# Wavelet mix on one Trainium2 core: the early unit's second products and edges run on one row half of the array beside projections on the other

## What is computed

```python
x: (8, 512, 207, 64)                      # batch, time, node, channel
a = x.transpose(0, 2, 3, 1).reshape(-1, 512)
for _ in range(3):                        # 8-tap filters, stride 2
    a, d = _dwt(a); details.append(d)
coeffs = [a] + details[::-1]
enh = [c * w[i] per channel for i, c in enumerate(coeffs)]
rec = enh[0]
for d in enh[1:]:
    rec = _idwt(rec[:, :d.shape[-1]], d)  # back to 512 samples
return x + rec(as b, t, n, c) @ proj_w.T + proj_b
```

## Time and profile before

| | |
|---|---|
| median of three runs | 2358.09 us |
| the profiled execution | 2359.12 us, its span 2357.3 us |
| PE busy | 2342.1 us (99% of the span) |
| PE weight loads busy | 2189.6 us (93%) |
| DVE busy | 1750.1 us (74%) |
| ACT busy | 1830.6 us (78%) |
| POOL busy | 284.2 us (12%) |
| a group in the middle of the run | 11.18 us |

### The profile page before, as it was taken

One profiled execution on the slowest core, in us unless ns is written; L12 is line 12 of the kernel. 1 busy time (PEld: TensorE's weight loads), 2 busy tenths in 40 slices (PEclk: granted clock), 3 DMA queues, 4 the chain that ended last, 5 costly groups with the idle time before them and its releaser, 6 DMA issues.

```text
span 2357.3 us, 85222 instructions
## 1 busy us (share of the span) xinstructions
PE 2342.1 (99%) x33980; PEld 2189.6 (93%) x33980; DVE 1750.1 (74%) x2920; ACT 1830.6 (78%) x3938; POOL 284.2 (12%) x1051
## 2 busy tenths in 40 slices
PE   9999999999999999999999999999999999999998
PEld 8999999999999999999999999999999999999987
DVE  5777777777777777777777777777777777777766
ACT  5777777777777777777777777777777777777776
POOL 1111111111111111111111111111111111111110
PEclk9999999999999999999999999999999999999998
DMA  3545454454644645444454644645445454544643
GB/s 127 219 184 191 178 201 173 182 212 162 242 162 162 233 172 199 180 188 186 178 203 170 235 162 162 241 163 210 183 174 198 178 192 182 222 162 167 237 162 122
DMA packets 107209, 439.42 MB, mean 186 GB/s; under 512 B 6801, under 2 KB 8081, under 8 KB 106898
## 3 DMA queue, kind: packets, MB, share of 16 engines
q1 hardware_dynamic: 106144, 434.16, 48.9%
q10 hardware_dynamic: 754, 0.28, 0.0%
HBM read 217.33 MB, written 217.06 MB: 184 GB/s over the span
## 4 chain that ended last, share of the span: by engine, by line
PE 98%; DVE 0%; issue 0%; DMA 0%; ACT 0%; ACTq 0%; DVEq 0%
PE proj_ps L436 31%; PE coefs_ps L382 31%; PE synth_ps L465 12%; PE synth_ps L477 11%; PE synth_ps L488 6%; PE proj_ps L446 2%; PE synth_ps L479 2%; PE synth_ps L467 2%; PE synth_ps L490 2%; DMA edge_sb<-edge_m 0%; DVE x_sb L676 0%; DVE proj_lo L656 0%; DVE coefs_sb L650 0%; ACT stack_sb L602 0%; ACTq L552 0%
## 5 line engine op out<-in xcount | busy, mean ns | idle before, releaser
L382 PEld LDWEIGHTS coefs_ps<-analysis_sb,x_sb 64*128 64x128 f32 x13200 | 945.5, 188 | 102.2 <-DVE coefs_sb L650 53.4
L382 PE MATMUL coefs_ps<-analysis_sb,x_sb 64*128 64x84 f32 x13200 | 1009.9, 270 | 2.7 <-DVE coefs_sb L645 1.5
L436 PE MATMUL proj_ps<-w_sb,coefs_sb 64*128 64x64 f32 x13248 | 871.3, 271 | 1.2 <-issue 1.2
L656 DVE TENSOR_TENSOR proj_lo<-proj_ps,proj_hi 128x512 fp32r<-128x512 f32 x828 | 568.1, 686 | 370.0 <-ACT proj_hi L571 370.0
L436 PEld LDWEIGHTS proj_ps<-w_sb,coefs_sb 64*128 64x128 f32 x13248 | 815.9, 189 | 1.4 <-issue 1.3
L650 DVE TENSOR_TENSOR coefs_sb<-coefs_ps,scale_sb 128x552 f32<-128x552 f32 x825 | 602.4, 730 | 207.6 <-PE coefs_ps L382 206.7
L571 ACT ACTIVATE proj_hi<-proj_ps 128x512 fp32r<-128x512 f32 x828 | 472.1, 596 | 174.6 <-PE proj_ps L446 157.4
L589 ACT ACTIVATE stack_sb<-proj_hi 20x512 fp32r<-20x512 f32 x621 | 390.9, 629 | 209.1 <-DVE proj_lo L656 204.1
L676 DVE TENSOR_TENSOR x_sb<-synth_ps,x_sb 128x512 f32<-128x512 f32 x828 | 531.7, 684 | 16.7 <-PE synth_ps L490 6.9
L341 POOL TENSOR_TENSOR coefs_sb<-coefs_sb 128x20 f32<-128x20 f32 x828 | 187.8, 227 | 1893.4 <-DVE coefs_sb L650 1892.7
L589 ACT ACTIVATE stack_sb<-proj_lo 20x512 fp32r<-20x512 f32 x621 | 390.4, 629 | 15.0
(11 more groups left out here) (58 smaller groups left out, 2849.1 us busy)
## 6 DMA issues: line engine op xcount, KB each, us to landing
x_sb<-x SPq DMA_DIRECT2D x182, 1152.0 KB, 11.7
out<-x_sb SPq DMA_DIRECT2D x182, 1152.0 KB, 6.3
out<-x_sb SPq DMA_DIRECT2D x1, 1280.0 KB, 4.7
x_sb<-x SPq DMA_DIRECT2D x1, 1024.0 KB, 8.5
out<-x_sb SPq DMA_DIRECT2D x2, 512.0 KB, 2.9
x_sb<-x SPq DMA_DIRECT2D x1, 768.0 KB, 5.7
x_sb<-x SPq DMA_DIRECT2D x1, 512.0 KB, 4.0
stack_sb<-bias_parts SPq DMA_DIRECT2D x12, 2.0 KB, 2.7
```

The lines of the kernel that those rows point to most:

```text
L382: return lambda cols: nc.tensor.matmul(out[:, at:at + HALF_COLS], x_sb[half_rows[side], w, cols], analysis_sb[half_rows[side], :], start=s ...
L436: mm = nc.tensor.matmul(out_cols[:, :, p, :], coefs_of(g, p)[rows, own_cols(w)], w_sb[rows, rows].rearrange("k (h c) -> k h c", h=2), star ...
L656: nc.vector.tensor_tensor(proj_lo[w][:, :].rearrange(by_node, n=2), proj_of(w)[:, :, 0:NODE_COLS], proj_hi[w][:, :].bitcast(fp32).rearrang ...
```

## The change

A new function, `synthesise_across(turn, g, half, behind)`, is called twice in a group, where `synthesise_second` of the early unit and the projections of windows 0 and 1 stood. A call makes the early unit's three second products and two edge products on row half `half`, and between them all eight matmuls that project windows 0 and 1 for node `1 - half`, which lie on the other half's rows. The second call does the same with the roles exchanged. `analyse_first` of pair 2 stands between the calls, `analyse_second` of pair 2 behind the second. The three first steps of the late unit now stand together ahead of `analyse_first` of pair 3, and `analyse_second` of pair 3 follows that directly. On DVE the tail's transpose moves ahead of the scaling of pair 1.

```diff
--- before.py
+++ after.py
@@ -491,6 +491,49 @@
                                           start=False, stop=stop, skip_group_check=True)
                 mm.then_inc(synthesised, 1)
 
+            def synthesise_across(turn, g, half, behind):
+
+
+                group, done = turn * GROUPS + g, (behind[0] * GROUPS + behind[1]) if behind else None
+                node = 1 - half
+                rows, own = half_rows[half], node_rows[node]
+                tiles = []
+                for w in UNITS[EARLY]:
+                    for p in range(PAIRS):
+                        tiles.append((w, p))
+
+                def project_next():
+                    w, p = tiles.pop(0)
+                    if p == 0 and node == 1:
+                        pe.wait_ge(lo_copied, group * WINDOWS + (PLACE[w] - 1))
+                        if w == ORDER[3]:
+                            pe.wait_ge(turned, group + 1)
+                    out_cols = proj_of(w)[:, node, 0:NODE_COLS].rearrange("k (h p c) -> k h p c", h=2, p=PAIRS)
+                    mm = nc.tensor.matmul(out_cols[:, :, p, :], coefs_of(g, p)[own, own_cols(w)],
+                                          w_sb[own, own].rearrange("k (h c) -> k h c", h=2),
+                                          start=True, stop=True, skip_group_check=True)
+                    if p == PAIRS - 1 and node == 0:
+                        mm.then_inc(projected, 1)
+
+                if behind:
+                    pe.wait_ge(half_synthesised, done * 2 + (EARLY + 1))
+                    bank = synth_ps[1 - half]
+                    for step, (weight, low, high) in enumerate(products(EARLY)):
+                        nc.tensor.matmul(bank[:, :], weight[rows, :], (high if half == 0 else low)[rows, :],
+                                         start=False, stop=False, skip_group_check=True)
+                        for _ in range((1, 2, 1)[step]):
+                            project_next()
+                    pe.wait_ge(edge_moved[2 if half == 0 else 1], (done + 1) * EDGE_MOVES)
+                    for weight, stop in ((edge_lo[:, :], False), (edge_hi[:, 0, :], True)):
+                        mm = nc.tensor.matmul(bank[:, :], weight[rows, :], stack_sb[EARLY][rows, :],
+                                              start=False, stop=stop, skip_group_check=True)
+                        if stop and half == 1:
+                            mm.then_inc(synthesised, 1)
+                        project_next()
+                        project_next()
+                while tiles:
+                    project_next()
+
             def turn_of(turn, first=False, last=False):
                 for g in range(GROUPS):
                     start = first and g == 0
@@ -515,18 +558,15 @@
                     if not start:
                         synthesise_first(*behind, EARLY, [0, 1, 2], False)
                     second_ahead(1)
-                    if not start:
-                        synthesise_second(*behind, EARLY)
+                    synthesise_across(turn, g, 0, None if start else behind)
                     first_ahead(2)
-                    project(turn, g, 0, [0, 1, 2, 3], first)
+                    synthesise_across(turn, g, 1, None if start else behind)
                     second_ahead(2)
-                    project(turn, g, 1, [0, 1, 2, 3], first)
                     if start:
                         pe.wait_ge(lo_built, 2)
                         pe.wait_ge(stacks_set, 16 * STACK_DMAS)
-                    synthesise_first(turn, g, LATE, [0], first)
+                    synthesise_first(turn, g, LATE, [0, 1, 2], first)
                     first_ahead(3)
-                    synthesise_first(turn, g, LATE, [1, 2], first)
                     second_ahead(3)
                     synthesise_second(turn, g, LATE)
 
@@ -695,8 +735,8 @@
                     scale_ahead(0)
                     split_low(turn, g, 2)
                     split_low(turn, g, 3)
+                    turn_tail(turn, g, first)
                     scale_ahead(1)
-                    turn_tail(turn, g, first)
                     add_behind(0)
                     add_behind(1)
                     scale_ahead(2)
```

## The result

The changed kernel takes 2670.1 us (median of 4 runs, 2667.7 to 2671.9), the kernel before in the same comparison 2359.1 us: 1.132 times as long, 95% interval 1.130 to 1.134. The forecast was 2663.

What follows compares the result with a forecast made beforehand. PE was taken as the bound, each row half paced by weight loads of 0.111 us. Terms 1.22 + 0.06 + 0.29 - 0.09 = 1.48 us a group, over 206 groups 305 us, gave 2663 us; 8-in-10 range 2570 to 2750.

Steps and rivals of the forecast that it cites:

- Step 1: Two calls: products on one half take 1.15 us, projections on the other 1.78, so each call lasts 1.78.
- Step 2: Late unit's wait for `summed`: the adding loses its cover, 1.22 us a group, plus 0.06 for order of issue.
- Step 3: Pair 3's analysis parts side by side: the second waits for PE's own signal, 0.29 us a group.
- Step 4: Group's first wait: DVE's scaling of pair 3 is ready in time with PE slower, gaining 0.09 us.
- Step 5: DVE's transpose ahead of scaling pair 1, and ACT's later copies of windows 0 and 1: both cost nothing.
- Sum: All terms per group: 1.48 us more in groups 1 to 206, 305 us in all.
- B: Rival on row-half loading: a lone half loads in 0.056 us, giving 2585 us; chance 0.12.
- C: Rival on PE's order: matmuls start strictly in program order whatever their half, giving 2712 us; chance 0.13.
- D: Rival on PE's clock: it falls when PE idles; 25 falls give 2750 us, more give 2900; chance 0.10.
- E: Rival at the two calls: faster, 2313 us, if lone loads take 0.056 us and `summed` is never awaited; chance 0.03.
- F: Rival on the two halves: fp32 and fp32r don't overlap across them, giving about 3160 us; chance 0.03.

Runs made afterwards that it cites:

- the adding cut: The change with DVE's adding of windows 0 and 1 cut to 32 of 512 columns: 2560.7 us.
- balanced calls: The change with one call whose halves swap products and projections after every step, in place of two calls: 2545.6 us.
- the late order alone: The kernel before with only the late unit's three first steps together, then both analysis parts of pair 3: 2400.6 us, ratio 1.018.
- 16 lone loads in a row: The kernel before with window 1's projections by node, four of node 1 alone, then four of node 0: 2433.3 us, ratio 1.032.
- the reversed late order: The change with the late unit's steps back in the order of the kernel before: 2666.4 us.
- the lone projections: The kernel before with both windows' projections by node, eight of node 1 then eight of node 0, no product beside them: 3273.0 us, one run.
- the early copy: The kernel before with ACT's copy of window 0's high part ahead of its four low tail moves: 2336.3 us, ratio 0.991.

## Why the prediction was right

By its steps:

- **Step 1, the two calls.** 16 loads in 1.78 us: half 1's run from 1019.72 to 1021.39 + 0.11 = 1021.50, 1.78. Call 2's first product load at T + 2.23: measured 1021.95 - 1019.71 = 2.24. The fifth product of call 2 was to start at T + 3.26; its recorded start, which is that of its predecessor's end, is 1022.99, T + 3.28.
- **Step 2, the adding.** Start at T + 3.71: measured 3.70. PE back at T + 5.05: measured 1024.81 - 1019.71 = 5.10. So the late unit is 1.27 us later, where the sum had 1.22 + 0.06. That this fits to 0.01 is luck: the 0.06 for the order of issue wasn't needed in the group shown, and the time from the additions' end to PE's load was 0.06 longer than the 0.05 that I had read from a load at the group's start. How the term splits, which the prediction left open, is from the experiments. With the adding cut, the late unit starts 0.96 us earlier; with balanced calls, and the whole adding, it starts 5.10 - 4.48 = 0.62 earlier. The two add up to more than 1.27, since they aren't separate shares: the imbalance makes the adding start late, and the adding is what ends last. Of the imbalance alone some 0.31 would be left (1.27 - 0.96).
- **Step 3, the signal.** 0.29 less the 0.09 of step 4: the late order alone cost 0.21.
- **Step 4.** 0.09; the wait's removal alone gave 0.10.
- **Step 5.** Nothing in the change, though 0.14 us by itself. Scaling 1 was to end at T + 1.41; it ends at 1020.34 + 0.73 = 1021.07, T + 1.36, half 0's first load for the analysis of pair 2 starts at 1021.12, and half 1 is busy until 1021.50. So the cover that the step named is there, though half 0 has hardly any of it to spare. ACT's later copies cost nothing that shows.
- **Sum.** 1.48 us a group predicted, 12.72 - 11.19 = 1.53 measured on the mean. A typical group (the median) takes 12.66 instead of 11.18, which is the 1.48. The 0.05 are 25 of the 170 groups that take about 13.0, 18 of them nine groups apart, so at one place of the turn, with a longer wait at the adding (1.0 instead of 0.7 us). Why it is that place I haven't found out.

The rivals: **B** (a lone half loads faster) falls by 16 lone loads in a row and by 2433 where it needed 2358. **C** (strictly in order) asked for 2712, and its term was 0.30 us in step 2: the additions start at T + 3.70, so that the term is nothing here, and C as I had priced it is out. But the price took for granted that half 0 starts call 2's projections with half 1's first product, at T + 2.34. It starts them at 1021.69, T + 1.98, with half 1's product load (1021.95) still to come, and 11 loads later is T + 3.20, ahead of the fifth product's T + 3.26. So strict order of the streams would have cost next to nothing, and the time doesn't test it. What the rows show is the loads: half 0 loads for its next analysis with three of half 1's projection loads to come, so in 182 of the 206 first calls. That agrees with the part of the rule cited from the Trainium skill (TensorE: Matmul & The Clock Gate, Part 3) that lets loads overlap running matmuls across row groups. The other part of that rule of the Trainium skill, that matmuls start and end in program order, is neither shown nor refuted: the recorded starts are out of that order (L512 at 1021.96, L522, which stands ahead of it, at 1021.98), but no row shows the true start of a stream. **D** didn't happen in the change (mean granted clock 0.998); in the lone projections the clock did fall, but with PE recorded as busy. **E** would have needed both of the things that failed. **F** falls by the balanced calls.

The expectations fared less well than the prediction: 2705 for the reversed late order, where I added the new wait to the kernel and forgot the first product that covers part of it; the total of the lone projections, where the clock fell; the cut adding, whose theory missed the new wait for DVE's scaling; and by a little the early copy and the balanced calls.

## What to carry to other kernels

Before packing unlike work on two row halves, add up each half's own time: in this kernel, where a half is paced by its weight loads, it gained nothing from a partner that rests, and a call lasted as long as its longer half. Then ask what the steps that move used to cover: here the projections behind the products hid 1.3 us of adding, and moving them beside the products exposed 0.96 of it. And when a wait is cut away to price it, look for the one that comes up behind it: here it took back nearly half of what the late unit had gained. A reordering that seems free (the transpose first, two dependent steps side by side) should be timed alone, since the change around it may hide its price.

## What the runs showed that I had not expected

The granted clock can fall in a kernel whose PE is recorded as busy. With both windows' projections on lone halves, PE was busy 97% of the long stretch and the clock was 0.82 on the mean, in stretches at 1.00 and at 0.50; with one window on lone halves it stayed at 1.00, and in the change, with PE busy 94% of the middle but a product beside most projections, at 0.998. It cost some 550 us by this estimate: the stretches at the lower level add up to 1112.6 us, and if they had run at twice the pace, the kernel would have taken about 2717, not 3273. What decides between the cases I didn't try to find out.

The second is how evenly a half runs ahead: 3 loads in the change, 3 to 4 in both kernels with lone halves, enough to smooth small differences between the halves and too few for a difference of 0.6 us in a call.
